# A node table filled by scatters from SBUF and loaded plainly, in place of an item table read by gathers

## The chip, the cores and the metric

The kernel runs on one core of a Trainium2 chip. The metric is the device time of one execution in microseconds (us). Five engines work side by side, each through its own list of instructions: TensorE (PE in the profile, its weight loads PEld), VectorE (DVE), ScalarE (ACT), GpSimd (POOL) and SyncE (SP). SP and ACT issue plain DMAs, POOL issues the indirect ones, in which a list of row numbers in SBUF picks the rows of a table in DRAM.

## What is computed

The reference is a chain of four layers on 3125 nodes with 256 features: a graph attention layer, a mixture of experts, a graph sum layer and an attention over slices. The change touches the second, and the first step of the third:

```python
x = x + _L0_gnn_ref(_layernorm(x), edge_index, ...)
x = x + _L0_ffn_ref(_layernorm(x)[None], router_w, w1, w2, w3)[0]
x = x + _L1_gnn_ref(_layernorm(x), L1_gnn_W, L1_gnn_b, edge_index)
x = x + _L1_ffn_ref(_layernorm(x)[None], ...)[0]

# _L0_ffn_ref, with 8 experts and the best 2 for each node
probs = softmax(flat @ router_w.T)
topk_probs, topk_idx = top_k(probs, 2)          # gates, made to sum to one
h = silu(flat w1[e]) * (flat w3[e])             # 682 wide
y = h w2[e]
out = sum over the two chosen e of gate[e] * y[e]
```

## The kernel before

Nodes are laid out as 25 tiles (`NT`) of 125 nodes (`P`), node = 125 x tile + partition. The residual stream `res` stays in SBUF. The phases follow one another, each a block with a barrier of all engines behind it: edges of the first graph layer, join, **router**, **experts**, **combine**, the sum over edges of the second graph layer, its node phase, and the last attention.

**Router** (`router_phase`). It normalises the nodes, stores the normalised rows to the DRAM table `xn_tab`, and chooses two experts for each node. Nodes are then grouped by expert into 56 items (`NI`) of 128 slots (`M`), an expert's last item being padded. `place[:, j, t]` is the slot of a node's j-th choice. From products of one-hot matrices, summed by TensorE in bank 2, VectorE makes `slot_token`, the node in each slot, in its last two instructions (L1461, L1462). 6250 of the 7168 slots hold a node.

**Experts** (`experts_phase`). GpSimd gathers the rows of each item from `xn_tab` into `e_x` (L1522, 56 indirect DMAs), with the first split of staged weights behind the sixteenth. A split (L1470, L1471) turns an expert's staged weights into a high and a low part; six more follow, each when a buffer is free. TensorE runs through the 56 items. At an item's end ScalarE copies the result from PSUM to one of two buffers `e_y` (L1645) and issues its store to the item table `y_tab` of 56 x 128 rows (L1647), 56 stores in all.

**Combine** (`combine_phase`). GpSimd clears a square, makes five small index rows (L842) and then issues 50 indirect DMAs (L1769): for each of 25 tiles and both choices the rows of `y_tab` at `place`, into `c_ys`. SP loads the last layer's weights (L1745 to L1756). VectorE clears the two halves of `sums` (L1784), then runs the walk (L869 to L896), small index work for the sum phase that has three products on TensorE in it, and then five groups of five tiles: wait for the group's ten gathers, ten multiply-adds into `res` (L1790), five statistics (L1793). Behind the fifth group come the normalising factors and 25 normalised tiles `c_xn` (L1254). SP stores them in five groups through `move` (L144, L145), which splits 125 partitions into 120 and 5. When they have landed, `close_layer` lets GpSimd clear the semaphores of the layer (L98), and the sum phase begins with its first gather (L930), the first of 392.

What a group of the combine stage waits for, and what it does:

```python
dve.wait_ge(ys_in[g], 16 * 2 * TB)
for j in range(2):
    for t in range(g * TB, (g + 1) * TB):
        m = v.scalar_tensor_tensor(out=k.res[:, t, :], in0=ys[:, j, t, :], scalar=k.gate[:, j, t:t + 1], in1=k.res[:, t, :], op0=ALU.mult, op1=ALU.add)
    me(dve, m)
```

The order on every engine is that of the code; no scheduler moves anything.

## Time and profile before

| what | us |
|---|---|
| median of 3 runs | 2197.47 (2193.42 to 2198.22) |
| the profiled execution, its own time | 2200.15 |
| its span, first to last instruction | 2198.4 |
| experts: first gather on GpSimd to last copy on ScalarE | 894.2 to 1307.2 |
| combine: first DMA on SP to the first gather of the sum phase | 1309.4 to 1403.6 |
| sum phase: first to last gather on GpSimd | 1403.6 to 1892.4 |

The span is cut by phases. Within a phase the question is which engine's list ends last, and what it waited for on the way. A row of a timeline gives the start of an instruction (or of a few merged ones) in us from the span's start, its length, the engine, the line in the kernel, what it writes and reads, how many were merged, and in square brackets how long the engine had idled before it and what ended that idle time. "issue" means that nothing which the profile shows was waited for. A Q behind an engine's name is its sequencer, which issues DMAs and sits at barriers.

### The profile page before, as it was taken

What the parts mean: (1) busy time and instruction counts of PE and PEld (TensorE: products, weight loads), DVE (VectorE), ACT (ScalarE), POOL (GpSimd) and SP (SyncE); (2) the same over time, 40 slices, a digit from 0 to 9 for tenths busy, and PEclk for the clock granted to TensorE, in tenths of its full rate; (3) what the DMA queues carried; (4) which work ended last, traced back from release to release, by engine and by line L of the source; (5) the groups of instructions that cost most, each with busy time, mean ns of one, the idle gap of its engine ahead of it and who ended that gap; (6) DMA issues with size and microseconds to landing.
All of it is one profiled execution on the core that took longest, in us unless ns stands there. A gap on an engine that the chain in (4) does not pass through costs nothing. (4 is left out here: it accounts for less than half of the span.)

```text
span 2198.4 us, 25811 instructions
## 1 busy us (share of the span) xinstructions
PE 1367.7 (62%) x6376; PEld 1110.0 (50%) x6377; DVE 955.0 (43%) x1910; ACT 447.7 (20%) x1239; POOL 1111.2 (51%) x1098
## 2 busy tenths in 40 slices
PE   2604676665652236798999971156656556477878
PEld 1403454544541225798999970134434444354557
DVE  8513544544434776432333335333323233365533
ACT  0213454444440011232333320000000000012210
POOL 4376777777746200574223117377777777303410
PEclk6756888777785665799999995577778787789979
DMA  5545889888878412242111023333333333100002
GB/s 131 141 119 160 295 301 312 283 279 264 282 236 180 42 40 59 88 154 96 60 60 60 21 63 104 108 105 105 105 105 105 105 105 105 57 1 0 0 0 59
DMA packets 151966, 268.97 MB, mean 122 GB/s; under 512 B 24036, under 2 KB 113476, under 8 KB 150763
## 3 DMA queue, kind: packets, MB, share of 16 engines
q0 software_dynamic: 46848, 127.07, 20.1%
q1 hardware_dynamic: 86760, 123.17, 17.1%
q10 hardware_dynamic: 18277, 17.70, 3.1%
q8 instruction: 44, 0.72, 0.1%
q14 instruction: 37, 0.30, 0.0%
HBM read 173.09 MB, written 94.74 MB: 122 GB/s over the span
## 5 line engine op out<-in xcount | busy, mean ns | idle before, releaser
L947 PE MATMUL bank<-sum_rows,sum_hot 128*125 x896 | 296.3, 496 | 281.6 <-SPq L921 216.3
L930 POOL DMA_INDIRECT sum_rows<-xn_tab,src_e x392 | 370.6, 945 | 148.3 <-issue 117.9
L721 POOL DMA_INDIRECT gat_rows<-xh_tab,src_e x364 | 344.3, 946 | 116.2 <-issue 107.5
L947 PEld LDWEIGHTS bank<-sum_rows,sum_hot 128*125 128x125 f32 x896 | 215.7, 251 | 362.3 <-issue 319.4
L778 PE MATMUL bank<-gat_rows,gat_same 128*128 128x264 f32 x784 | 255.4, 478 | 92.9 <-DVE gat_rows L754 92.9
L968 DVE TENSOR_TENSOR sums<-sums,bank 125x256 f32 x224 | 93.9, 421 | 348.9 <-PE bank L947 333.7
L778 PEld LDWEIGHTS bank<-gat_rows,gat_same 128*128 128x128 f32 x784 | 177.7, 241 | 131.7 <-issue 98.2
L1562 PE MATMUL bank<-weights,e_xthigh 128*128 x896 | 220.7, 330 | 11.1 <-POOL weights L1471 7.5
L800 ACT COPY gat_outs<-bank 128x264 f32<-128x264 f32 x392 | 148.4, 379 | 163.1 <-PE bank L778 150.4
L1691 DVE TENSOR_TENSOR e_h<-e_gated,bank 128x342 f32<-128x342 f32 x112 | 57.1, 510 | 269.2 <-ACT e_gated L1633 269.2
L1562 PEld LDWEIGHTS bank<-weights,e_xthigh 128*128 128x128 f32 x896 | 154.0, 192 | 20.6 <-issue 20.5
L1562 PE MATMUL bank<-weights,e_xtlow 128*128 x448 | 144.6, 323 | 0.0
L1583 PE MATMUL bank<-weights,e_hthigh 128*128 (+2 forms) x672 | 134.2, 296 | 0.2 <-DVE e_htlow L1696 0.2
L1220 ACT COPY n_xt<-bank 128x250 f32<-128x250 f32 x25 | 8.0, 372 | 572.0 <-PE bank L1207 571.6
L754 DVE TENSOR_TENSOR gat_rows<-gat_rows,bank 128x1792 f32<-128x1792 f32 x56 | 110.7, 2017 | 14.5 <-ACT bank L797 14.5
L1522 POOL DMA_INDIRECT e_x<-xn_tab,slot_token x56 | 54.6, 975 | 108.9 <-POOLq L1263 84.2
L1470 POOL CAST weights<-staged 128x4264 fp32r<-128x4264 f32 x7 | 26.3, 3758 | 153.0 <-SPq L1515 153.0
L1583 PEld LDWEIGHTS bank<-weights,e_hthigh 128*128 128x128 f32 (+2 forms) x672 | 103.1, 190 | 0.5 <-issue 0.4
L1633 ACT ACTIVATE e_gated<-bank 128x342 f32<-128x342 f32 x112 | 51.0, 455 | 245.2 <-PE bank L1562 245.2
L1583 PE MATMUL bank<-weights,e_htlow 128*128 x336 | 94.2, 280 | 0.0
L1562 PEld LDWEIGHTS bank<-weights,e_xtlow 128*128 128x128 f32 x448 | 86.0, 192 | 0.0
L1972 POOL TENSOR_TENSOR t_logit<-t_logit,t_peak 125x512 f32<-125x512 f32 x25 | 26.1, 1045 | 81.6 <-DVE t_peak L2131 81.6
(457 smaller groups left out, 2324.6 us busy)
## 6 DMA issues: line engine op xcount, KB each, us to landing
parts<-gat_outs SPq DMA_DIRECT2D x28, 1904.0 KB, 8.3
staged<-w_tab SPq DMA_DIRECT2D x8, 2132.0 KB, 8.4
w_tab<-w_stage SPq DMA_DIRECT2D x16, 682.0 KB, 10.6
w_raw<-in_L_ffn_w_dram SPq DMA_DIRECT2D x16, 640.0 KB
y_tab<-e_y ACTq DMA_DIRECT2D x56, 128.0 KB, 1.7
gat_rows<-xh_tab,src_e POOLq DMA_INDIRECT x392
sum_rows<-xn_tab,src_e POOLq DMA_INDIRECT x392, 2.7
w_tab<-w_stage SPq DMA_DIRECT2D x8, 768.0 KB
```

The source lines that it names most:

```text
L721: pool.indirect_dma_start(out=rows[b % R][:, t, :], out_offset=None, in_=k.xh_tab, in_offset=bass.IndirectOffsetOnAxis(ap=k.src_e[:, b * S ...
L754: v.tensor_tensor(f, f, weight[:, t0 * H:t1 * H].rearrange("p (t h a) -> p t h a", h=H, a=1).to_broadcast([EP, SB // 2, H, D]), ALU.mult). ...
L778: nc.tensor.matmul(k.ps[1 + (s * SB + t) % BK][:, 0:sums_w], same[s % 2][:, t, :], rows[s][:, t, 0:sums_w], start=True, stop=True).then_in ...
L800: nc.scalar.copy(outs[s % 2][:, t, 0:sums_w], k.ps[1 + (s * SB + t) % BK][:, 0:sums_w]).then_inc(taken, 1)
L930: pool.indirect_dma_start(out=rows[:, at // IP % (RING * GPAIRS), at % IP, :], out_offset=None, in_=k.xn_tab, in_offset=bass.IndirectOffse ...
L947: m = nc.tensor.matmul(k.ps[s][0:P, 0:C], hot[u][:, s, c, :], rows[:, bass.ds(slot, 1), c, :].rearrange("p a c -> p (a c)"), start=(c == 0 ...
L968: v.tensor_tensor(into, into, k.ps[s][0:P, 0:C], ALU.add).then_inc(added, 1)
L1522: pool.indirect_dma_start(out=x[:, i, :], out_offset=None, in_=k.xn_tab, in_offset=bass.IndirectOffsetOnAxis(ap=k.slot_token[:, i:i + 1], ...
L1562: last = nc.tensor.matmul(bank[:, 0:HH[a]], xt[s][px][:, c, :], part(slot, up_at(m, pw, c) + HB[a], 128, HH[a]), start=(n == 0), stop=(n = ...
L1583: m = nc.tensor.matmul(DOWN[s][:, 0:C], ht[a][ph][0:rows, b, :], part(slot, down_at(pw, 3 * a + b), rows, C), start=(a == 0 and n == 0), s ...
L1633: nc.scalar.activation(gated[a][:, 0:HH[a]], UP[a][:, 0:HH[a]], ACT.Silu).then_inc(silued, 1)
L1691: v.tensor_tensor(h[a][:, 0:HH[a]], gated[a][:, 0:HH[a]], GATE[a][:, 0:HH[a]], ALU.mult).then_inc(h_made, 1)
```

## The change

The item table becomes a node table of two rows for each node: row n for the first choice of node n, row 3125 + n for the second. The router makes a second list from the same products, `slot_row`, the node-table row of each slot. For that the second choice's column numbers run on from 25, the lane number goes in plus one (`row1`), so that an empty slot is told by zero, and five more VectorE instructions turn the sum into both lists. An empty slot gets a row number beyond the table. In the experts phase ScalarE copies an item's result over the item's own input `x[:, i, :]`; it issues no store. GpSimd scatters the 56 items to the node table behind its last split, and SP waits for all of them before the phase ends. In the combine phase SP loads the first choices and ACT the second ones, in five groups each, plainly; GpSimd clears `sums` where VectorE did.

```diff
-    k.xn_tab, k.y_tab = k.dram("xn_tab", [N, C]), k.dram("y_tab", [NI * M, C])
+    k.xn_tab, k.y_tab = k.dram("xn_tab", [N, C]), k.dram("y_tab", [2 * N, C])
...
+            me(dve, v.tensor_scalar(row1[:, :], k.node[:, 0:1], 1.0, None, ALU.add))
...
-                me(dve, v.tensor_scalar(at_item[:, at, 1, :], of_place[:, :, :], k.node[:, 0:1], None, ALU.mult))
+                me(dve, v.tensor_scalar(at_item[:, at, 1, :], of_place[:, :, :], row1[:, 0:1], None, ALU.mult))
...
-            me(dve, v.scalar_tensor_tensor(out=k.slot_token[:, :], in0=k.ps[2][:, 0:NI], scalar=float(P), in1=token[:, :], op0=ALU.mult, op1=ALU.add))
+            me(dve, v.scalar_tensor_tensor(out=token[:, :], in0=k.ps[2][:, 0:NI], scalar=float(P), in1=token[:, :], op0=ALU.mult, op1=ALU.add))
+
+            me(dve, v.tensor_scalar(second[:, :], token[:, :], float(N) + 0.5, -float(N), ALU.is_gt, ALU.mult))
+            me(dve, v.scalar_tensor_tensor(out=second[:, :], in0=token[:, :], scalar=-1.0, in1=second[:, :], op0=ALU.add, op1=ALU.add))
+            me(dve, v.tensor_scalar(k.slot_token[:, :], second[:, :], 0.0, None, ALU.max))
+            me(dve, v.tensor_scalar(second[:, :], token[:, :], 0.5, 4.0 * N, ALU.is_lt, ALU.mult))
+            me(dve, v.scalar_tensor_tensor(out=k.slot_row[:, :], in0=token[:, :], scalar=-1.0, in1=second[:, :], op0=ALU.add, op1=ALU.add))
...
+            sp.wait_ge(y_out, 16 * NI)
...
+            for i in range(NI):
+                pool.wait_ge(y_kept, i + 3)
+                pool.indirect_dma_start(out=k.y_tab, out_offset=bass.IndirectOffsetOnAxis(ap=k.slot_row[:, i:i + 1], axis=0),
+                                        in_=x[:, i, :], in_offset=None, bounds_check=2 * N - 1, oob_is_err=False).then_inc(y_out, 16)
...
-                if i >= 2:
-                    act.wait_ge(y_out[s], 16 * (i // 2))
-                nc.scalar.copy(y[s][:, :], DOWN[s][:, 0:C]).then_inc(y_kept, 1)
-                act.wait_ge(y_kept, i + 3)
-                act.dma_start(rows[i], y[s][:, :]).then_inc(y_out[s], 16)
+                nc.scalar.copy(x[:, i, :], DOWN[s][:, 0:C]).then_inc(y_kept, 1)
...
+            for g in range(GROUPS):
+                move(sp, ys[:, 0, g * TB:(g + 1) * TB, :], y_rows[:, 0, g * TB:(g + 1) * TB, :], ys_in[g])
...
-            for t in range(NT):
-                for j in range(2):
-                    pool.indirect_dma_start(out=picked[:, j, t, :], out_offset=None, in_=k.y_tab,
-                                            in_offset=bass.IndirectOffsetOnAxis(ap=k.places[:, j, t:t + 1], axis=0)).then_inc(ys_in[t // TB], 16)
+            for half in k.sums:
+                nc.gpsimd.memset(half[:, :, :], 0.0)
...
+            for g in range(GROUPS):
+                move(act, ys[:, 1, g * TB:(g + 1) * TB, :], y_rows[:, 1, g * TB:(g + 1) * TB, :], ys_in[g])
             norm_roots(k, act, deviations, roots)
...
-            for half in k.sums:
-                v.memset(half[:, :, :], 0.0)
             k.walk.on_vector(dve)
             for g in range(GROUPS):
-                dve.wait_ge(ys_in[g], 16 * 2 * TB)
+                dve.wait_ge(ys_in[g], 64)
```

GpSimd's list, from its last split in the experts phase to the first gathers of the sum phase, before:

```order
L1470 CAST weights<-staged 128x4264
L1471 TENSOR_TENSOR weights<-staged,weights 128x4264
L1481 UNCONDITIONAL_BRANCH
L1763 UNCONDITIONAL_BRANCH
L1765 MEMSET att_square 128x512
L842 IOTA walk_bound 24x1
L842 IOTA walk_pair_row 128x196
L842 IOTA walk_item_row 128x224
L842 IOTA walk_item_col 110x2
L842 IOTA walk_pair_col 98x2
L1769 DMA c_ys<-y_tab,place 128x256 x50
```

and the same stretch now:

```order
L1477 CAST weights<-staged 128x4264
L1478 TENSOR_TENSOR weights<-staged,weights 128x4264
L1538 DMA y_tab<-e_x,slot_row 6250x256 x56
L1488 UNCONDITIONAL_BRANCH
L1769 UNCONDITIONAL_BRANCH
L1771 MEMSET att_square 128x512
L842 IOTA walk_bound 24x1
L842 IOTA walk_pair_row 128x196
L842 IOTA walk_item_row 128x224
L842 IOTA walk_item_col 110x2
L842 IOTA walk_pair_col 98x2
L1774 MEMSET sums 125x6400 x2
```

The 56 scatters stand between the last split and the barrier (the two branches), and two clears stand where 50 gathers stood. On SP the combine phase began, before, with

```order
L1740 UNCONDITIONAL_BRANCH
L1745 DMA att_w_x<-in_L_ffn_W_x_dram 128x2x512
L1745 DMA att_w_fx<-in_L_ffn_W_fx_dram 128x2x512
L1745 DMA att_w_out<-in_L_ffn_W_out_dram 128x4x256
L1746 DMA att_b_fx<-in_L_ffn_b_fx_dram 1x512
```

and it begins now with

```order
L1744 UNCONDITIONAL_BRANCH
L144 DMA c_ys<-y_tab 120x5x256
L145 DMA c_ys<-y_tab 5x5x256
...
L144 DMA c_ys<-y_tab 120x5x256
L145 DMA c_ys<-y_tab 5x5x256
L1751 DMA att_w_x<-in_L_ffn_W_x_dram 128x2x512
L1751 DMA att_w_fx<-in_L_ffn_W_fx_dram 128x2x512
```

with five such pairs ahead of the weights; ACT has five pairs too, ahead of its square root. The end of the router on VectorE was

```order
L1459 TENSOR_SCALAR load_after<-r_sums 1x8
L1461 COPY r_token<-bank 128x56
L1462 SCALAR_TENSOR_TENSOR slot_token<-bank,r_token 128x56
```

and is

```order
L1460 TENSOR_SCALAR load_after<-r_sums 1x8
L1462 COPY r_token<-bank 128x56
L1463 SCALAR_TENSOR_TENSOR r_token<-bank,r_token 128x56
L1465 TENSOR_SCALAR r_second<-r_token 128x56
L1466 SCALAR_TENSOR_TENSOR r_second<-r_token,r_second 128x56
L1467 TENSOR_SCALAR slot_token<-r_second 128x56
L1468 TENSOR_SCALAR r_second<-r_token 128x56
L1469 SCALAR_TENSOR_TENSOR slot_row<-r_token,r_second 128x56
```

five rows longer, with both lists made in it. The semaphores that GpSimd clears behind the combine phase are 53, from 50.

## Rows read from the trace of the kernel before

**Rows 1.** Instruction groups by line, 1309 to 1404: busy, mean ns | idle before, releaser.

```profile
L1769 POOL DMA_INDIRECT c_ys<-y_tab,place x50 | 48.5, 970 | 15.1 <-issue 15.1
L1790 DVE SCALAR_TENSOR_TENSOR res<-c_ys,gate,res 125x256 f32<-125x256 f32 x50 | 20.7, 480 | 20.1 <-DMA c_ys<-y_tab,place 19.9
```

**Rows 2.** Timeline of VectorE in the combine phase.

```profile
1322.83 0.29 DVE L869 TENSOR_SCALAR walk_past<-bank,walk_bound 24x196 f32<-24x196 f32 x1
...
1328.60 0.27 DVE L886 CAST walk_pair_i<-walk_pair 1x224 int32<-1x224 f32 x1
...
1332.57 4.17 DVE L1790 SCALAR_TENSOR_TENSOR res<-c_ys,gate,res 125x256 f32<-125x256 f32 x10
...
1338.42 4.16 DVE L1790 SCALAR_TENSOR_TENSOR res<-c_ys,gate,res 125x256 f32<-125x256 f32 x10
...
1376.14 4.17 DVE L1790 SCALAR_TENSOR_TENSOR res<-c_ys,gate,res 125x256 f32<-125x256 f32 x10 [6.75 <-DMA c_ys<-y_tab,place]
...
1382.03 0.08 DVE L463 MEMSET rstd<- 125x25 f32 x1
```

**Rows 3.** GpSimd's gathers of the sum phase: ns min/median/max, first and last start.

```profile
L930 POOL DMA_INDIRECT sum_rows<-xn_tab,src_e x392: 942/946/962, 1403.6 to 1892.4; - x196
```

**Rows 4.** Timelines of SP, TensorE and GpSimd as the combine phase begins.

```profile
1309.42 0.40 SPq L1745 DMA_DIRECT2D att_w_x<-in_L_ffn_W_x_dram  x1
...
1309.48 1.65 PE L851 MATMUL bank<-dst_e,ident 128*128 128x392 f32 x2 [2.69 <-PEq L1481]
...
1310.63 0.13 POOL L842 IOTA walk_pair_col<- 98x2 f32 x1
```

**Rows 5.** Tile view of `adst_edge`: an earlier phase's 25 scatters, with bounds.

```profile
L611 POOL DMA_INDIRECT adst_edge<-xh,start_row x25: 1188/1189/2167, 96.3 to 133.2; - x25
...
DMA to landing us min/median/max: 2.4/3.8/7.3
```

**Rows 6.** GpSimd's last instruction of the experts phase, in its timeline.

```profile
1209.49 9.37 POOL L1471 TENSOR_TENSOR weights<-staged,weights 128x4264 fp32r<-128x4264 f32 x1
```

**Rows 7.** Tile view of `e_y`: the copies of the 56 results on ScalarE.

```profile
L1645 ACT COPY e_y<-bank x56: 372/373/376, 915.6 to 1306.8; 128x256 f32<-128x256 f32 x56
```

**Rows 8.** Timeline of ScalarE: the last copy and the last store of the experts phase.

```profile
1306.83 0.37 ACT L1645 COPY e_y<-bank 128x256 f32<-128x256 f32 x1 [2.16 <-PE bank L1583]
1307.23 0.33 ACTq L1647 DMA_DIRECT2D y_tab<-e_y  x1
```

**Rows 9.** DMA view: issues, KB each, median us to landing.

```profile
y_tab<-e_y ACTq DMA_DIRECT2D x56, 128.0 KB, 1.7
```

**Rows 10.** Timeline of VectorE at the end of the router.

```profile
892.54 0.22 DVE L1461 COPY r_token<-bank 128x56 f32<-128x56 f32 x1
892.79 0.22 DVE L1462 SCALAR_TENSOR_TENSOR slot_token<-bank,r_token 128x56 int32<-128x56 f32 x1
```

**Rows 11.** DMA view of 8 to 24, `res` loaded: packets, MB, share of 16 engines.

```profile
q10 hardware_dynamic: 2861, 2.89, 95.5%
```

**Rows 12.** Windows: us, busy of PE, PEld, DVE, ACT, POOL; PEclk, DMA share, GB/s.

```profile
1389.00:1392.00 3.00, 0.00 (x0) 0.00 (x0) 2.99 (x10) 0.00 (x0) 0.00 (x0) 0.50 0.97 310
```

**Rows 13.** Timeline of the first phase: two clears by GpSimd.

```profile
0.81 0.52 POOL L289 MEMSET srcq_i<- 98x512 int32 x1 [0.29 <-POOLq L2257]
1.27 0.52 POOL L290 MEMSET dstq_i<- 98x512 int32 x1
```

**Rows 14.** Timeline of the attention phase: VectorE beside GpSimd, and apart from it.

```profile
2006.45 1.29 DVE L1254 TENSOR_SCALAR t_xn<-res,mv,rstd 125x256 f32 x1 [0.15 <-issue]
2006.55 1.04 POOL L1976 TENSOR_TENSOR t_logit<-t_logit,t_total 125x512 f32<-125x512 f32 x1
...
2069.12 0.41 DVE L1254 TENSOR_SCALAR t_xn<-res,mv,rstd 125x256 f32 x1
```

**Rows 15.** Timeline of the spread phase: scans on VectorE, gathers on GpSimd.

```profile
145.78 9.04 DVE L654 TENSOR_TENSOR_SCAN filled<-cont_q,sparse 98x512 f32<-98x512 f32 x8
...
148.06 1.93 POOL L618 DMA_INDIRECT gat_rows<-xh_tab,src_e  x1 [0.30 <-issue]
```

18 lines of the change are left out of this document (7 added, 11 removed).

## The prediction

> **What bounds the kernel now.** I began with the stages in time, then asked in each stage that the diff touches which list ends last. The groups by line of the combine stage show GpSimd issuing 50 gathers and VectorE's 50 multiply-adds idle for 20.1 us, 19.9 of it for those gathers [rows 1]. One gather costs 0.97 us busy and 0.30 idle, (48.5 + 15.1) / 50 = 1.27 us, so ten for a group cost 12.7 us, against 1338.42 - 1332.57 = 5.85 us of VectorE work for a group [rows 1, 2]. From the third group on the stage goes at GpSimd's pace; its fifth group starts at 1376.14 and ends at 1382.03 [rows 2]. Ahead of the groups VectorE clears the two halves of `sums`, and the walk begins only at 1322.83, 13.4 us after the stage's first DMA [rows 2, 4]. The phases stand behind one another, and the sum phase is one row of 392 gathers at GpSimd's pace, (1892.4 - 1403.6) / 391 = 1.25 us each [rows 3]; it doesn't shorten, but it starts as much earlier as the combine stage ends, and so does all that follows. What is won between 1309 and 1382 is won in the total, unless the router or the experts phase gives it back.
>
> **The combine stage.** All 50 gathers go. The clears go from VectorE to GpSimd. The walk needs the index rows (ready at 1310.76) and the first product (1309.48 + 1.65 = 1311.13) [rows 4], so its first step can start at 1311.2 in place of 1322.83: 11.6 us earlier.
>
> GpSimd clears 2 x 6400 numbers a partition beside the walk. Its rate is in two clears of 512 that start 0.46 us apart [rows 13]: 6400 x 0.46 / 512 = 5.75 us each, from 1310.8 to 1322.3. Does VectorE work on beside them? One VectorE instruction took 1.29 us in place of 0.41, and ended at 2007.74, 0.15 after a GpSimd instruction that ran from 2006.55 to 2007.59 [rows 14]. So a GpSimd instruction can hold VectorE until its own end. In the walk the candidates are five short steps from the cast on (L886), which read and write SBUF with one operand and no PSUM. Moved up by 11.6 the cast comes at 1317.0, after the second clear has begun at about 1316.5; held, it goes on at 1322.3, 5.3 us later. That is a bound from above; the bound from below is 0, since the row is of a GpSimd instruction that reads SBUF, and a clear doesn't. I take the 5.3: it is the only case in these rows of long GpSimd work beside such steps.
>
> The Trainium skill states this as a rule (SBUF — State Buffer, section "Who interferes with whom"): a VectorE copy, cast or scalar operation in a two-port mode and any GpSimd instruction exclude each other, and the one issued second waits for the whole of the first. By it the 5.3 us are due; by the same page VectorE instructions with two SBUF inputs are held only by GpSimd work that reads, so the multiply-adds would not be. The trace agrees for [rows 14]; for a clear no row shows it.
>
> So the first group starts at 1332.57 - 11.6 + 5.3 = 1326.3, and five groups at VectorE's pace end at 1326.3 + 5 x 5.85 = 1355.5, if the rows are there. They are 2 x 3.2 = 6.4 MB, loaded plainly in pieces of 1 KB by SP and ACT. The nearest row is the load of `res`, of the same shape and through the same helper: 2.89 MB in 16 us with the 16 engines 95.5% busy, 181 GB/s [rows 11]. At that the last group lands at 1309.4 + 2 + 35.4 = 1346.8, ahead of 1326.3 + 4 x 5.85 = 1349.7, when VectorE asks for it. Stores of the same groups went at 310 GB/s [rows 12], which would land it at 1332. Either way the load is covered, down to 6.4 MB / 38.3 us = 167 GB/s. The last layer's weights now stand behind five pairs of loads on SP; they are not needed before the node phase, and SP's next timed duty, the store of the first normalised group, comes at about 1358. ACT's square root waits only for VectorE at 1356, behind its own five pairs. The combine stage thus ends 1382.03 - 1355.5 = 26.5 us earlier. Three more semaphores are cleared than the 50 of before. They are cleared somewhere between 1382.03 and 1403.6 [rows 2, 3], a stretch that is mostly normalising and storing: at most 3/50 of its 21.6 us, 1.3 us, at least nothing; I take 0.2.
>
> **The experts phase.** The 56 stores leave ScalarE, which is not late there, at no gain. The 56 scatters stand behind the last split, which ends at 1209.49 + 9.37 = 1218.9 [rows 6]. By then, at (1306.8 - 915.6) / 55 = 7.11 us an item [rows 7], some 43 of 56 results are made: GpSimd has a backlog. The one scatter in this trace, 25 times with bounds, takes 1.19 us [rows 5], with starts (133.2 - 96.3) / 24 = 1.54 us apart over all, the slow first one (2.17) included. 56 x 1.54 = 86.2 us, ending at 1305.1. The last result is copied at 1306.83 + 0.37 = 1307.2 [rows 8]. So the backlog is just gone, with 2 us to spare; the limit is (1307.2 - 1218.9) / 56 = 1.58 us a scatter. Bounds: 1.25 us, the gathers' pace [rows 3], and 1.93 + 0.30 = 2.23, which gathers took beside VectorE's scans [rows 15]. I take 1.54, as the nearest; VectorE's work in this phase has one operand in PSUM, and is no scan.
>
> Not hidden is the last scatter. Before, the store issued at 1307.23 landed 1.7 us later [rows 8, 9], 1308.9, and the next phase began at 1309.42. A scatter takes 2.4 to 7.3 us to landing, 3.8 in the middle [rows 5]: 1307.2 + 3.8 + 0.5 = 1311.5, 2.1 us later. From below 0.7; from above 5.6, where the backlog is not quite gone or the queue is full.
>
> **The router.** Five VectorE instructions behind the list's last one, at 892.79 - 892.54 = 0.25 us apart [rows 10], and one more near its start: 1.5 us, all on the path, since the experts phase begins with the gathers that read the list. The other edits there change numbers, not instructions.
>
> **Sum.** -26.5 + 2.1 + 1.5 + 0.2 = -22.7 us. The profiled execution's own time is 2200.15, which makes 2177.5; it lies 2.7 above the median of the runs, 2197.47. From the median: 2197.5 - 22.7 = 2174.8.
>
> **The rivals.**
> A: the clears hold nothing. For it: a clear reads nothing. Then the first group starts at 1321.0, the groups could end at 1350.2, and by the load at 181 GB/s the fifth starts at 1346.8 and ends at 1352.7. Saved are 29.3 to 31.8, less 3.8: 2166 to 2172 (some 2170).
>
> B: the load becomes the bound. For it: two queues ask for rows of one table at once, and [rows 11] has the engines at 95% already at 181 GB/s. At three quarters of it, 136 GB/s, the load takes 47 us, the fifth group starts at 1358.5 and ends at 1364.4: 17.6 saved, less 3.8, 2183.7. Against it: the 310 GB/s of [rows 12], with the same groups.
>
> C: GpSimd doesn't keep pace. Each 0.1 us a scatter over 1.58 adds 5.6 us to the experts phase. At 1.7 the total is 2181.5.
>
> D, the other side: the same mechanism far enough. At 2.23 us a scatter [rows 15] GpSimd ends at 1218.9 + 124.9 = 1343.8 and the phase at about 1346: it starts the combine stage 34 us later than my forecast has it, which is 2209, 12 us slower than before. It decides from 1.58 + 22.7 / 56 = 1.99 us on. Against it: the gathers of the same phase ran beside the same VectorE work at no visible cost.
>
> E: the change doesn't do what it says, because VectorE waits elsewhere or the sum phase starts late for a reason that I don't see: within 0.2%.
>
> **How the numbers follow.** Forecast 44%, A 27%, B 12%, C 8%, D 5%, E 4%. The range: from 2164, A at its best with the runs' own spread of some 2 us, to 2184, B at three quarters. It leaves out D, E and the far parts of B and C. 0.2% is 4.4 us, about what a measurement of this kernel can tell from no change. Faster by more: forecast, A, B and most of C, 0.90; within it: E, 0.04; slower: D and a little, 0.06.
>
> **What would show it.** In the profile after: scatters 1.5 us apart from 1220 to 1305, the last one waiting for ScalarE; combine's first DMA at about 1313 (1309.4 + 1.5 + 2.1); the walk's first step 2 us behind it, and the cast (L886) late by some 5 us behind GpSimd's second clear; five groups 5.85 us apart with no wait for DMA; the sum phase's first gather at about 1381. It is wrong if the scatters end well behind ScalarE's last copy, if the groups wait for `c_ys`, or if the sum phase's gathers are no longer 1.25 us apart.

## The result: 5.4 us of a forecast 22.7

| | before | after |
|---|---|---|
| median of the runs, us | 2196.74 (12 runs, 2192.98 to 2199.21) | 2191.38 (12 runs, 2186.87 to 2197.60) |
| profiled execution, its own time / span | 2200.15 / 2198.4 | 2193.07 / 2191.3 |
| granted TensorE clock, mean | 0.781 | 0.784 |

The ratio is 0.9976, with a 95% interval from 0.9966 to 0.9986. The kernel became faster by a quarter of a percent; forecast were 2174.8 us and a range from 2164 to 2184. In the last three comparisons of the study the kernel before itself took 2528 to 2559 us, at a mean granted clock of 0.72 to 0.73, so the totals of those runs are set against that before alone and rank no cure, and their traces serve for durations, waits and the lengths of stages.

The two profiles differ by 7.1 us of span. Where they differ, in us from the span's start:

| event | before | after | difference of the stretch |
|---|---|---|---|
| first gather of the join stage | 663.8 | 669.2 | +5.4 |
| experts stage, ScalarE's first cast | 893.6 | 902.2 | +3.2 |
| ScalarE's last copy of a result ends | 1307.2 | 1314.8 | -1.0 |
| combine stage, SP's first DMA | 1309.4 | 1326.0 | +9.0 |
| first group of multiply-adds | 1332.6 | 1344.8 | -4.4 |
| fifth group's statistics end | 1382.0 | 1374.1 | -20.2 |
| first gather of the sum phase | 1403.6 | 1396.6 | +1.0 |
| end | 2198.4 | 2191.3 | -0.2 |

The combine stage has its gain: from its first DMA to the sum phase's first gather 94.1 us before, 70.6 now. But it begins 16.6 us later: 7.6 of these were lost ahead of the last copy, where the change has only the router's six instructions, and 9.0 between the last copy and the next stage.

VectorE in the combine stage of the kernel after, in its timeline (start us, duration us, engine, line, operation, [idle before <- releaser]); these rows answer to [rows 2], with L1794 for L1790:

```profile
1327.84 0.41 DVE L869 TENSOR_SCALAR walk_past<-bank,walk_bound 24x196 f32<-24x196 f32 x1 [14.95 <-PE bank L851]
...
1330.55 7.69 DVE L877 TENSOR_SCALAR walk_diag<-ident,walk_at 110x110 f32<-110x110 f32 x2
...
1344.83 4.17 DVE L1794 SCALAR_TENSOR_TENSOR res<-c_ys,gate,res 125x256 f32<-125x256 f32 x10
...
1350.69 4.16 DVE L1794 SCALAR_TENSOR_TENSOR res<-c_ys,gate,res 125x256 f32<-125x256 f32 x10
...
1368.21 4.15 DVE L1794 SCALAR_TENSOR_TENSOR res<-c_ys,gate,res 125x256 f32<-125x256 f32 x10
...
1374.08 0.08 DVE L463 MEMSET rstd<- 125x25 f32 x1
```

The groups run 5.83 to 5.86 us apart, and the fifth has no wait in brackets, where [rows 2] had 6.75 us of it. The walk begins 1.8 us behind the stage's first DMA, as forecast. One pair of its steps, L877, takes 7.69 us; in other runs below it takes 0.46.

GpSimd from its last split through the stage's start. The scatters (L1538) answer to [rows 5], the index rows to [rows 4]:

```profile
1216.85 9.37 POOL L1478 TENSOR_TENSOR weights<-staged,weights 128x4264 fp32r<-128x4264 f32 x1
1226.38 1.04 POOL L1538 DMA_INDIRECT y_tab<-e_x,slot_row  x1 [0.17 <-issue]
1227.72 1.00 POOL L1538 DMA_INDIRECT y_tab<-e_x,slot_row  x1 [0.30 <-issue]
...
1291.64 0.97 POOL L1538 DMA_INDIRECT y_tab<-e_x,slot_row  x1 [0.31 <-issue]
1298.19 0.97 POOL L1538 DMA_INDIRECT y_tab<-e_x,slot_row  x1 [5.58 <-ACT e_x L1653]
1305.26 0.97 POOL L1538 DMA_INDIRECT y_tab<-e_x,slot_row  x1 [6.09 <-ACT e_x L1653]
1312.01 0.97 POOL L1538 DMA_INDIRECT y_tab<-e_x,slot_row  x1 [5.78 <-ACT e_x L1653]
1315.62 0.97 POOL L1538 DMA_INDIRECT y_tab<-e_x,slot_row  x1 [2.63 <-ACT e_x L1653]
1326.05 0.53 POOL L1771 MEMSET att_square<- 128x512 f32 x1 [9.46 <-POOLq L1488]
...
1327.14 0.13 POOL L842 IOTA walk_item_col<- 110x2 f32 x1
1327.24 0.13 POOL L842 IOTA walk_pair_col<- 98x2 f32 x1
1327.32 5.42 POOL L1774 MEMSET sums<- 125x6400 f32 x1
```

The scatters go 1.28 us apart, 52 of them follow each other without a wait, the backlog is worked off at 1292.6, and the last four wait for ScalarE, each behind its own result. The costly row is the first of L1771: L1488 is the block of the experts stage, POOLq GpSimd's sequencer, and between the end of the last scatter, 1316.59, and the next stage lie 9.46 us. The waits of SP say who was late there (waited for: us in total, times, longest us):

```profile
SPq L1488 <- DMA y_tab<-e_x,slot_row: 104.7, 1, 104.7
SPq L1488 <- PEq L1488: 8.1, 1, 8.1
```

SP waited for the scatters to land, and then 8.1 us more at the end of the block for the other engines. So the rows had landed at 1326.0 - 8.1 = 1317.9, some 2 us behind the issue of the last scatter. It wasn't the data that was late. Nor was it TensorE, whose last product ended at 1314.4, or ScalarE, whose last row is:

```profile
1314.47 0.37 ACT L1653 COPY e_x<-bank 128x256 f32<-128x256 f32 x1 [2.23 <-PE bank L1594]
```

The router's five added steps, behind the one of [rows 10], which is now the first row here:

```profile
900.19 0.22 DVE L1463 SCALAR_TENSOR_TENSOR r_token<-bank,r_token 128x56 f32<-128x56 f32 x1
900.44 0.19 DVE L1465 TENSOR_SCALAR r_second<-r_token 128x56 f32<-128x56 f32 x1
...
901.37 0.22 DVE L1469 SCALAR_TENSOR_TENSOR slot_row<-r_token,r_second 128x56 int32<-128x56 f32 x1
```

And the gathers of the edge phase, whose code is the same in both kernels, first before and then after (ns min/median/max, first and last start us):

```profile
L721 POOL DMA_INDIRECT gat_rows<-xh_tab,src_e x364: 942/946/1022, 183.8 to 637.7; - x182
```

```profile
L721 POOL DMA_INDIRECT gat_rows<-xh_tab,src_e x364: 952/957/1048, 183.8 to 641.6; - x182
```

Each takes 11 ns longer at the median, and the quickest 10 ns. It is the same for the other gathers ahead of the experts stage, 471 with these 364 (25 of windows, 28 in the spread phase, 50 in the join stage; the other 4 of the spread phase take 3 ns more); the 25 scatters of L611 take what they took. From the experts stage on both kernels have 946 again, the 392 gathers of the sum phase (L930) too: 1396.6 to 1885.6, 489.0 us, as in [rows 3].

So three things were to be explained: who holds the walk, why GpSimd is late at the end of the experts stage, and why gathers ahead of any change are slower. All kernels that were run for it, each with the ratio to before in the same comparison:

| kernel | median us (runs) | before there | ratio, 95% interval |
|---|---|---|---|
| after_last_two | 2188.87 (7) | 2195.68 | 0.9956 (0.9941 to 0.9972) |
| after_small_clears | 2196.82 (12) | 2195.68 | 1.0005 (0.9994 to 1.0016) |
| before_row_tile | 2197.03 (11) | 2195.68 | 1.0003 (0.9994 to 1.0012) |
| after_old_table | 2191.01 (8) | 2195.68 | 0.9976 (0.9964 to 0.9988) |
| before_end_gather | 2202.14 (12) | 2198.48 | 1.0023 (1.0013 to 1.0032) |
| before_end_scatter | 2205.89 (6) | 2198.48 | 1.0038 (1.0023 to 1.0053) |
| last_two_late_clears | 2184.59 (6) | 2198.48 | 0.9944 (0.9929 to 0.9958) |
| last_two_act_clears | 2184.42 (6) | 2198.48 | 0.9939 (0.9924 to 0.9955) |
| after_spare_rows | 2564.11 (6) | 2527.71 | 1.0149 (1.0116 to 1.0183) |
| late_clears_spare_rows | 2550.90 (6) | 2527.71 | 1.0092 (1.0063 to 1.0122) |
| after_late_clears | 2550.62 (8) | 2527.71 | 1.0086 (1.0058 to 1.0115) |
| before_end_scatter_free | 2523.21 (12) | 2527.71 | 0.9979 (0.9961 to 0.9997) |
| after_late_clears, second time | 2594.98 (4) | 2558.16 | 1.0152 (1.0128 to 1.0175) |
| last_two_first | 2585.04 (4) | 2558.16 | 1.0108 (1.0085 to 1.0131) |
| after_last_28 | 2555.56 (12) | 2558.16 | 0.9993 (0.9978 to 1.0008) |
| before_end_narrow | 2566.00 (12) | 2558.16 | 1.0039 (1.0018 to 1.0061) |
| after_late_clears, third time | 2594.97 (5) | 2558.51 | 1.0154 (1.0136 to 1.0173) |
| before_node_scatter | 2558.02 (10) | 2558.51 | 0.9997 (0.9984 to 1.0010) |

The last ten rows say something against the change. Every kernel in them that issues 54 or 56 scatters behind the last split took 0.9 to 1.5% longer than before, though its combine stage is as short as in the other traces. The traces place it in the experts stage, while the backlog of scatters goes out. Windows of that time (us, then busy us of PE, PEld, DVE, ACT and POOL with instructions, PEclk, DMA share, GB/s), of the kernel after, and of after_late_clears, third time:

```profile
1226.00:1285.00 59.00, 59.00 (x421) 57.20 (x421) 20.47 (x60) 20.08 (x68) 45.06 (x47) 1.00 0.26 92
```

```profile
1442.00:1500.00 58.00, 18.11 (x90) 15.87 (x89) 3.70 (x11) 3.39 (x11) 43.12 (x45) 0.60 0.26 91
```

Beside the same stream of scatters TensorE is busy all the time in the one, and 18.1 of 58.0 us in the other, idle at "issue", that is, for nothing that the profile shows, once for 14.9 us. The DMA engines moved 91 GB/s beside it, against 92. The granted clock was 1.00 (2.4 GHz) until 1453, with TensorE idle since 1450, and 0.50 (1.2 GHz) for the rest of the window. Eight results took 109 us there in place of 56, and the stage from its first gather to its last copy 502 us; it took 449 to 456 us in the three kernels of these rows with one scatter or none in it, and 465 in after_last_28 with 28. Why TensorE idles, no run shows, and the kernel after itself wasn't among these runs; after_late_clears differs from it in the place of the clears alone.

### The profile page after: what moved, and what is told of

It is laid out like the page before. It is cut to its first block and busy times, and to the rows that moved or that the text cites. A ratio compares the mean times of both kernels' runs of the same rounds, so it can differ in the third digit from the quotient of the medians.

```text
span 2191.3 us, 25791 instructions
## 1 busy us (share of the span) xinstructions
PE 1364.0 (62%) x6376; PEld 1106.4 (50%) x6377; DVE 955.0 (44%) x1914; ACT 448.0 (20%) x1239; POOL 1131.9 (52%) x1106
## 5 line engine op out<-in xcount | busy, mean ns | idle before, releaser
L930 POOL DMA_INDIRECT sum_rows<-xn_tab,src_e x392 | 370.8, 946 | 177.7 <-issue 116.7
L721 POOL DMA_INDIRECT gat_rows<-xh_tab,src_e x364 | 348.2, 957 | 116.2 <-issue 107.9
L1573 PEld LDWEIGHTS bank<-weights,e_xthigh 128*128 128x128 f32 x896 | 153.9, 192 | 20.3 <-issue 20.2
L1538 POOL DMA_INDIRECT y_tab<-e_x,slot_row x56 | 54.6, 974 | 35.8 <-ACT e_x L1653 20.1
```

The source lines that it names most:

```text
L721: pool.indirect_dma_start(out=rows[b % R][:, t, :], out_offset=None, in_=k.xh_tab, in_offset=bass.IndirectOffsetOnAxis(ap=k.src_e[:, b * S ...
L930: pool.indirect_dma_start(out=rows[:, at // IP % (RING * GPAIRS), at % IP, :], out_offset=None, in_=k.xn_tab, in_offset=bass.IndirectOffse ...
L1538: pool.indirect_dma_start(out=k.y_tab, out_offset=bass.IndirectOffsetOnAxis(ap=k.slot_row[:, i:i + 1], axis=0), in_=x[:, i, :], in_offset= ...
L1573: last = nc.tensor.matmul(bank[:, 0:HH[a]], xt[s][px][:, c, :], part(slot, up_at(m, pw, c) + HB[a], 128, HH[a]), start=(n == 0), stop=(n = ...
```

## Experiments on the end of the experts stage

**after_last_two** issues the last two scatters in the next stage, ahead of the clears; SP and ScalarE wait for them there before their first loads:

```diff
-            for i in range(NI):
-                pool.wait_ge(y_kept, i + 3)
-                pool.indirect_dma_start(out=k.y_tab, ...
+            for i in range(NI - 2):
+                pool.wait_ge(y_kept, i + 3)
+                scatter(pool, i)
 ...
             k.walk.on_pool(pool)
+            k.last_rows(pool)
+            nc.gpsimd.memset(k.att["square"][:, :, :], 0.0).then_inc(squares0, 1)
 ...
+            act.wait_ge(k.y_out, 16 * NI)
             for g in range(GROUPS):
                 move(act, ys...
```

> The kernel after, with the scatters of the last two items moved behind the walk's index rows in the combine stage (SP's and ScalarE's loads there wait for them, and the experts stage ends when 54 have landed). In after the combine stage begins 11.2 us behind ScalarE's last copy, though the DMA queues are silent from 2.8 us behind it on. Theory 1, what is late is GpSimd itself, at the end of a block that it leaves behind an indirect DMA: with its last scatter of the block 7 us ahead of the last copy, the combine stage begins about 2 to 3 us behind the last copy, its loads start 3.5 to 5 us behind its own start, and the total falls by 9 less up to 2.6, by which the clears come later and let the walk go later: 2182 to 2186. Theory 2, a scatter's completion comes late: the combine stage begins as early, but its loads start 10 to 12 us behind its start; the total is then 2185 to 2192. Theory 3, the late start has nothing to do with the scatters: the stage still begins 11 us behind the last copy, 2191 or more.

ScalarE's last copy and GpSimd's timeline there:

```profile
1310.66 0.37 ACT L1659 COPY e_x<-bank 128x256 f32<-128x256 f32 x1 [2.16 <-PE bank L1600]
```

```profile
1301.51 0.97 POOL L1540 DMA_INDIRECT y_tab<-e_x,slot_row  x1 [6.03 <-ACT e_x L1659]
1311.79 0.12 POOL L842 IOTA walk_bound<- 24x1 f32 x1 [9.31 <-POOLq L1488]
```

The stage now begins 0.8 us behind the end of the last copy, 1311.03, in place of 11.2, and GpSimd shows 9.31 us between its last scatter and the stage, though its rows had landed 7.1 us before the stage. Its loads start at 1316.16, 4.4 us behind the stage's start: theory 1; a slow completion (theory 2) would have put them at 1322 or later. The stage itself is 73.2 us long in place of 70.6, since the clears come 2.4 us later. Expected were 2182 to 2186 us, measured 2188.87, with a profiled run of 2186.44: the trace has the mechanism, the median gives back less of it, and the interval of its ratio overlaps with that of after (0.9966 to 0.9986).

Is it any indirect DMA, or a scatter? Two kernels add one instruction to the kernel before, behind ScalarE's last copy, which SP waits for. **before_end_gather**:

```diff
+            pool.wait_ge(y_kept, NI + 2)
+            pool.indirect_dma_start(out=x[:, 0, :], out_offset=None, in_=k.xn_tab,
+                                    in_offset=bass.IndirectOffsetOnAxis(ap=k.slot_token[:, NI - 1:NI], axis=0)).then_inc(tail, 16)
```

> The kernel before, with one more gather on GpSimd at the end of the experts block: it waits for ScalarE's last copy, reads 128 rows of xn_tab into a tile that nothing reads any more, and SP waits for it. In after the next stage began 9.5 us behind the end of GpSimd's last scatter, in after_last_two 9.3 us. Theory 1, GpSimd takes some 9 us to leave a block behind any indirect DMA: the gather ends at about 1308.3, the combine stage begins at about 1317.7 in place of 1309.4, total 8 us over before, 2204. Theory 2, about 5 us, as behind the spread stage's gathers (178.2 to 183.8): 1313.5, total 2200. Theory 3, only scatters cost it: the stage waits for the landing alone and begins at about 1311, total 2197 to 2198.

**before_end_scatter**:

```diff
+            pool.wait_ge(y_kept, NI + 2)
+            pool.indirect_dma_start(out=k.spare_tab, out_offset=bass.IndirectOffsetOnAxis(ap=k.slot_token[:, NI - 1:NI], axis=0),
+                                    in_=y[(NI - 1) % 2][:, :], in_offset=None, bounds_check=N - 1, oob_is_err=False).then_inc(tail, 16)
```

> The same with a scatter in place of the gather: the last item's result to a spare table of 1 KB rows that nothing reads, with bounds. Theory 1 and theory 3: the combine stage begins at about 1317.8. It also asks why every indirect DMA ahead of the experts stage takes 957 ns in after and 946 in before, with tiles and tables in the same place or not: if a scatter of 1 KB rows somewhere in the program does it, the edge phase's gathers (L721) take 957 ns here too and the total is 2208 to 2209; if it is another part of the change, 946 ns and 2204.

GpSimd's timeline in the one and in the other:

```profile
1308.88 0.98 POOL L1532 DMA_INDIRECT e_x<-xn_tab,slot_token  x1 [88.77 <-ACT e_y L1650]
1315.06 0.53 POOL L1770 MEMSET att_square<- 128x512 f32 x1 [5.20 <-POOLq L1481]
```

```profile
1314.08 1.04 POOL L1533 DMA_INDIRECT spare_tab<-e_y,slot_token  x1 [89.14 <-ACT e_y L1651]
1320.10 0.53 POOL L1771 MEMSET att_square<- 128x512 f32 x1 [4.97 <-POOLq L1482]
```

Neither theory 1 (9 us) nor theory 3 (scatters alone) stands: one indirect DMA as GpSimd's last work of the block costs some 5 us, be it a gather (5.20) or a scatter (4.97). What makes 9.46 of it? **after_spare_rows** takes away the bounds and the rows that they leave out: it gives each empty place a row of its own behind the table.

```diff
-            me(dve, v.tensor_scalar(second[:, :], token[:, :], 0.5, 4.0 * N, ALU.is_lt, ALU.mult))
+            me(dve, v.scalar_tensor_tensor(out=second[:, :], in0=token[:, :], scalar=0.5, in1=spare[:, :], op0=ALU.is_lt, op1=ALU.mult))
 ...
-                                        in_=x[:, i, :], in_offset=None, bounds_check=2 * N - 1, oob_is_err=False).then_inc(y_out, 16)
+                                        in_=x[:, i, :], in_offset=None).then_inc(y_out, 16)
```

> The kernel after, where the rows of empty places (some 16 of 128 an item) go to rows of their own behind the table's 6250 in place of being left out by the bounds, so that the scatters need no bounds. GpSimd needed 9.46 us to leave the block in after and 9.31 in after_last_two, but 5.20 behind one gather at the end and 4.97 behind one scatter with bounds and no row out of them. Theory 1, the bounds or the rows left out make the difference: here the leaving takes about 5.0 us, the combine stage begins 4.4 us earlier, and if bounds also make the indirect DMAs ahead of the experts stage slow (957 ns), these take 946 again, 5 us more: 2182 to 2187. Theory 2, the number of scatters does it: 9.4 us, 957 ns, 2191.

```profile
1558.05 0.96 POOL L1540 DMA_INDIRECT y_tab<-e_x,slot_row  x1 [2.57 <-ACT e_x L1655]
1568.47 0.53 POOL L1773 MEMSET att_square<- 128x512 f32 x1 [9.46 <-POOLq L1490]
```

9.46 us to the hundredth: bounds have no part in it. late_clears_spare_rows (below) has the same change. **after_last_28** halves the number. ScalarE's plain stores fill the table's rows before that, and the routed rows of the first 28 items are left out of the result:

```diff
-            for i in range(NI):
+            pool.wait_ge(filled, 16 * 49)
+            for i in range(28, NI):
                 pool.wait_ge(y_kept, i + 3)
 ...
+                if i < 28:
+                    act.wait_ge(y_kept, i + 3)
+                    for at in (i, i + 28):
+                        rows = min(M, 2 * N - at * M)
+                        if rows > 0:
+                            act.dma_start(k.y_tab[at * M:at * M + rows, :], x[0:rows, i, :]).then_inc(filled, 16)
```

> The kernel after, in which GpSimd scatters the last 28 items alone; the rows of the first 28 are stored plainly by ScalarE into all of the table's rows before that, 49 stores, so that the routed rows of these items are left out of the result. GpSimd leaves the block in 9.46 us behind 56 scatters, in 9.31 behind 54, in 4.97 behind one: (9.46 - 4.97) / 55 = 0.082 us a scatter. Theory 1, it goes with the number of scatters: here 4.97 + 27 x 0.082 = 7.2 us. Theory 2, it goes with what the last few did (their spacing and their rows are as in after): 9.4 us.

```profile
1542.41 0.97 POOL L1539 DMA_INDIRECT y_tab<-e_x,slot_row  x1 [2.58 <-ACT e_x L1654]
1550.56 0.53 POOL L1778 MEMSET att_square<- 128x512 f32 x1 [7.17 <-POOLq L1488]
```

7.17 where 7.2 was expected. One scatter 4.97, 28 scatters 7.17, 54 scatters 9.31, 56 scatters 9.46: 4.9 us and 0.082 for each scatter of the block, an estimate from these four. Gathers don't count in this way: before_end_gather had 57 of them in the block, at 5.20. Nor is the count the whole rule: the spread phase has 25 scatters of 32-byte rows, with 28 gathers behind them, and leaves in 5.59. What GpSimd does in this time, no row shows.

## Experiments on the held walk

**after_small_clears** cuts each clear into 25 instructions:

```diff
             for half in k.sums:
-                nc.gpsimd.memset(half[:, :, :], 0.0)
+                for t in range(NT):
+                    nc.gpsimd.memset(half[:, t, :], 0.0)
```

> The kernel after, with GpSimd's two clears of 6400 numbers a partition cut into 50 clears of 256. Theory 1, a GpSimd clear holds a VectorE step of the walk until its own end (in after, L877 took 7.7 us in place of 0.5, up to the end of the second clear): a held step is let go after at most 0.3 us, the first group of multiply-adds starts about 12.5 us behind the stage's first DMA in place of 18.8, and the total is 5.5 to 6.5 us under after, about 2185. Theory 2, the walk is late for another reason (the loads' descriptors, or VectorE shares the port with whatever GpSimd writes, whole or in pieces): the first group still starts 17 to 19 us behind, total 2191.

VectorE's held step, and GpSimd's clears:

```profile
1330.99 9.62 DVE L877 TENSOR_SCALAR walk_diag<-ident,walk_at 110x110 f32<-110x110 f32 x2
```

```profile
1327.76 12.72 POOL L1775 MEMSET sums<- 125x256 f32 x50
```

My theory 1 falls in its detail. The step isn't let go at the end of the clear in hand, 0.25 us later, but at the end of the fiftieth: VectorE had no turn between clears that follow one another without a gap. The 50 take 12.7 us in place of 10.8, and the hold grows by these 1.9. (The trace explains 2.1 us of stage; the median is 5.4 over after's, and the rest isn't explained.) In the kernel after it was the same with two: L877 came at 1330.55 during the first clear and ended at 1338.2, with the second.

**last_two_late_clears** puts both clears behind the walk, on top of after_last_two:

```diff
+            pool.wait_ge(walked, 1)
             for half in k.sums:
                 nc.gpsimd.memset(half[:, :, :], 0.0)
```

> after_last_two with GpSimd's two clears behind the end of the walk, so that they lie beside the multiply-adds and statistics in place of the walk. There the walk's L877 was held for 11.4 us, until the second clear was through. Theory 1, multiply-adds and statistics are not held: the first group starts about 10.4 us behind the stage's first index row in place of 21.3, the fifth waits 1 or 2 us for its rows, total 9 to 10 us under after_last_two, 2179 to 2180. Theory 2, something in a group (the multiply-adds with a scale from SBUF, or the statistics) is held as L877 was, until both clears are through: the first group still starts early, but the second starts 6 to 11 us late, total 2183 to 2189.

VectorE's timeline, with GpSimd's clears below it:

```profile
1316.38 0.46 DVE L877 TENSOR_SCALAR walk_diag<-ident,walk_at 110x110 f32<-110x110 f32 x2
...
1326.47 4.17 DVE L1806 SCALAR_TENSOR_TENSOR res<-c_ys,gate,res 125x256 f32<-125x256 f32 x10 [3.06 <-DMA c_ys<-y_tab]
1330.67 1.73 DVE L1809 BATCH_NORM_STATS2 stats<-res 125x6 f32<-125x256 f32 x5
1333.14 4.17 DVE L1806 SCALAR_TENSOR_TENSOR res<-c_ys,gate,res 125x256 f32<-125x256 f32 x10 [0.73 <-DMA c_ys<-y_tab]
...
1352.02 4.17 DVE L1806 SCALAR_TENSOR_TENSOR res<-c_ys,gate,res 125x256 f32<-125x256 f32 x10 [0.81 <-DMA c_ys<-y_tab]
```

```profile
1323.52 10.81 POOL L1784 MEMSET sums<- 125x6400 f32 x2 [7.44 <-DVEq L1801]
```

L877 takes 0.46 us, and a group beside the clears takes as long as one without them, 4.17 and 1.73. So multiply-adds and statistics aren't held. But of the 10.1 us by which the walk ends earlier (21.3 to 11.1 us behind the stage's start) the stage keeps 4.9 (73.21 to 68.36 us from its start to the sum phase's first gather): groups now wait for their rows, 3.06, 0.73, 0.17 and 0.81 us. The last rows are there 35.4 us behind the first load, 6.4 MB at 181 GB/s. This is the load that [rows 11] gave, and it becomes the bound as soon as the walk no longer is. The total, 2184.59, is 4.3 us under after_last_two, where 9 to 10 were expected; by the ratios, 0.9944 and 0.9956 of their own before, it is 2.6 us, with intervals that overlap.

**last_two_act_clears** gives the clears to ScalarE:

```diff
+            for half in k.sums:
+                nc.scalar.mul(half[:, :, :].rearrange("p t c -> p (t c)"), k.ones[0:P, 0:1].to_broadcast([P, NT * C]), 0.0)
             norm_roots(k, act, deviations, roots)
```

> after_last_two with the two clears on ScalarE, behind its issues of loads (two multiplications by zero of 6400 numbers a partition, from one column of ones). ScalarE has nothing to do there until the square root. Theory 1, ScalarE holds nobody: the first group starts about 10.4 us behind the stage's first index row, the total is 9 to 10 us under after_last_two, 2179 to 2180, the same as last_two_late_clears at its best. Theory 2, the clears end behind the square root's turn (they begin only when the issues are through, some 24 us behind the stage's start): 2182 to 2186.

ScalarE cleared for 10.96 us, from 1339.69, and was through 12 us ahead of its square root. The total, 2184.42, is the same as with late clears, and for the same reason; the groups waited 3.03, 0.44, 1.17, 0.59 and 1.02 us for rows. Both are about 0.6% faster than before and a third of a percent faster than after; they are the best of this study.

**after_late_clears** has the late clears alone (the same edit, without the moved scatters), and was run three times:

> The kernel after, with GpSimd's clears behind the end of the walk and nothing else. The walk is let go 7.2 us earlier, the first group could start at about 1337.6. In last_two_late_clears, where the walk was through 8 us behind the first load, the groups then waited for their rows: 6.4 MB took 35.4 us, 181 GB/s. Theory 1: the first group starts 11.6 us behind the stage's first DMA or with a short wait, the fifth some 35.5 us behind it, and the gain over after is 6 to 7 us, 2184.5 to 2185.5. Theory 2, the loads' wait eats more than half of it: 2188 or more.

VectorE's held step in the first one's trace:

```profile
1581.74 0.47 DVE L877 TENSOR_SCALAR walk_diag<-ident,walk_at 110x110 f32<-110x110 f32 x2
```

This is the cleanest evidence on the walk, since nothing but the place of the clears differs from after, and the loads run beside the step as they do there: 0.47 us in place of 7.69, and as much in the two other traces. The first group starts at 1588.93, 11.7 us behind the stage's first DMA, with 0.16 us of wait; the fifth waits 0.57 us for its rows, and the sum phase begins 64.9 us behind the stage's start in place of 70.6 (64.4 and 64.5 in the others). Theory 1 has the walk right; what it is worth in a total isn't measured, since the three totals, 0.9 to 1.5% over before, are those of the stalled TensorE told above.

**last_two_first** is last_two_late_clears with the two scatters ahead of the index rows:

> last_two_late_clears (2184.6 us) with the last two scatters ahead of the walk's index rows on GpSimd in place of behind them. The loads, for which the first group there waited 3.06 us and later groups 1.7 more, start 0.9 us earlier; the walk starts 2.4 us later, which is less than that wait. Theory 1, the loads are what ends last: 0.9 us less, about 2183.7. Theory 2, the walk becomes it: 0 to 1 us more, 2185.

The first group waits 0.16 us there, and from ScalarE's last copy to the sum phase's first gather it takes 68.7 us in place of 69.1: less than half of the 0.9 that theory 1 had. The total, 1.0108 of before, says nothing of it.

**late_clears_spare_rows** adds the edit of after_spare_rows to last_two_late_clears:

> The same beside the two cures already run: last two scatters in the combine stage, clears behind the walk (last_two_late_clears, 2184.6 us), and no bounds. With the last two scatters moved the leaving is hidden at 9.3 us as at 5, so theory 1 gives only what the gathers ahead of the experts stage give back: 2180 if they take 946 ns again, 2184.6 if they stay at 957.

Its gathers ahead of the experts stage took 960 ns, so nothing was given back; its total, 1.0092 of before, is one of those with the stalled TensorE.

## Experiments on the gathers ahead of the change

**before_row_tile** is the kernel before with the tile that the change allocates; **after_old_table** is the kernel after with the table at its old length:

```diff
-    k.slot_token = k.sb("slot_token", [M, NI], I32)
+    k.slot_token, k.slot_row = k.sb("slot_token", [M, NI], I32), k.sb("slot_row", [M, NI], I32)
```

```diff
-    k.xn_tab, k.y_tab = k.dram("xn_tab", [N, C]), k.dram("y_tab", [2 * N, C])
+    k.xn_tab, k.y_tab = k.dram("xn_tab", [N, C]), k.dram("y_tab", [NI * M, C])
```

> The kernel before, with one thing of the change alone: the tile slot_row (56 numbers a partition) is allocated behind slot_token and never used, so that every tile behind it lies 224 bytes higher. In the profile after, the edge phase's gathers (L721) take 957 ns at the median mean in place of 946, the join phase starts 5.4 us later and the experts phase 8.6 us later, of which six VectorE instructions of the router explain 1.5. Theory 1, the place of the tiles in SBUF does it: here the gathers take 957 ns, the join phase starts at about 669 us in place of 663.8, the experts phase at about 900.5 in place of 893.6, and the total is 4 to 7 us over before (2201 to 2204). Theory 2, something else does it (the shorter table, or the code): 946 ns, 663.8 us, 893.6 us, and the total of before, 2197, within 2 us.

> The kernel after, with y_tab allocated at its old 7168 rows (the last 918 unused), so that the tables behind it in DRAM (dst_pad, start_tab, parts, chains) lie where they lay before. Theory 1 (place of the tiles in SBUF): nothing changes against after, gathers 957 ns, join phase at about 669, 2191 us. Theory 2 (place of the tables in DRAM): gathers 946 ns, join phase at about 664, experts phase at about 895, total 2185 to 2187.

The medians of L721 were 947 and 957 ns, the totals those of before and of after. Both theories fall: neither the place of the tiles nor that of the tables does it. before_row_tile shows something else. Its experts stage began at 897.5, 3.9 us later than in the profile of before, with quick gathers and the same median time. So of two single profiles some 2 to 4 us ahead of the experts stage mean nothing.

before_end_scatter (above) had 960 ns, and before_end_gather, with its gather in the same place, 946. One scatter at the end of the experts stage is enough, though the gathers that are slower with it run 576 to 1282 us ahead of it, so it can't be its transfer that slows them. **before_end_scatter_free** leaves out its bounds (its diff is against before_end_scatter), **before_end_narrow** takes rows of 8 numbers, and **before_node_scatter** has such a scatter in the node stage in place of the experts stage:

```diff
-                                    in_=y[(NI - 1) % 2][:, :], in_offset=None, bounds_check=N - 1, oob_is_err=False).then_inc(tail, 16)
+                                    in_=y[(NI - 1) % 2][:, :], in_offset=None).then_inc(tail, 16)
```

```diff
+            pool.indirect_dma_start(out=k.spare_tab, out_offset=bass.IndirectOffsetOnAxis(ap=k.slot_token[:, 0:1], axis=0),
+                                    in_=k.ones[:, 0:H], in_offset=None, bounds_check=N - 1, oob_is_err=False).then_inc(tail, 16)
+            pool.wait_ge(tail, 16)
```

> before_end_scatter without bounds on its one scatter. There the gathers ahead of the experts stage took 958 to 960 ns in place of 946, with nothing changed up to them, and the total was 7 us over before. Theory 1, a scatter with bounds on rows of 1 KB does it: here 946 ns, and a total some 4 to 5 us under before_end_scatter, 2201 to 2202. Theory 2, any scatter of such rows does it: 957 to 960 ns, 2206.

> before_end_scatter with rows of 32 bytes in place of 1 KB, into a spare table of 8 numbers a row. Theory 1, the length of the row makes the indirect DMAs ahead of the experts stage slow: here they take 946 ns, and the total is 4 to 5 us under before_end_scatter's 2206, at 2201 to 2202, as before_end_gather. Theory 2, any scatter in or behind the experts stage does it: 957 to 960 ns, 2206.

> The kernel before, with one scatter of 128 rows of 32 bytes on GpSimd in the node stage, behind the last gather of the program (its semaphore is waited for on GpSimd, beside the stage's weights). Theory 1, a scatter slows the indirect DMAs ahead of it in the program by some 11 ns each: here all of them, the 392 gathers of the sum stage (L930) among them, take 957 ns in place of 946, and the total is some 9 us over before. Theory 2, only those of the first layer's stages are slowed: 957 there and 946 from the experts stage on, total 5 us over before. Theory 3, it goes with the experts stage itself: 946 everywhere, total of before.

L721 (here L722) in before_end_narrow, and in before_node_scatter:

```profile
L722 POOL DMA_INDIRECT gat_rows<-xh_tab,src_e x364: 954/960/997, 197.2 to 778.5; - x182
```

```profile
L722 POOL DMA_INDIRECT gat_rows<-xh_tab,src_e x364: 940/946/957, 197.7 to 774.4; - x182
```

Without bounds it was 958 ns. So it is neither the length of the row nor the bounds, and a scatter behind the sum phase does nothing at all: theory 3 of the last one, it goes with a scatter in the experts stage. Other stages weren't tried, and this scatter differs from before_end_narrow's in its source and its index column too. What carries it from there to the gathers of the first layer, no run shows. It stays open, with its size known: in the edge phase the first to the last gather take 457.9 us in after and 458.5 in before_end_scatter, 453.9 in before. That is 3.9 us in after; the slower gathers ahead of the edge phase cost nothing, since it begins at 183.8 in both.

## Why the prediction missed, step by step

The sum was -26.5 + 2.1 + 1.5 + 0.2 = -22.7. The profiles give -7.1, the medians -5.4.

**The gathers that go, and the pace of a group: right.** The 50 gathers and VectorE's 19.9 us of waiting for them are gone, the groups go 5.83 to 5.86 us apart, and the walk starts 11.6 us earlier against the stage's start, as worked out.

**The load: right.** In the kernel after no group waits for rows, so rival B is out here; last_two_late_clears shows how near the bound was, with the 181 GB/s of [rows 11].

**The hold of VectorE: right in kind, wrong in place and size.** The working let the five short steps from the cast on (L886) be held, by 5.3 us. Held was L877, 7.2 us (7.69 less 0.46), so rival A is out. The step that failed is the list of candidates, "five short steps from the cast on": L877 also reads one operand from SBUF and writes SBUF, and it comes beside the first clear. The Trainium skill (SBUF — State Buffer, section "Who interferes with whom") would have pointed at it: it names copies, casts and `tensor_scalar` as the operations that can take the shared pair of ports, and leaves out the form that writes its accumulator. The trace agrees: L873, of that form, ran in 0.41 us beside the same clear, L877 didn't. It says that who issues first has the ports for the whole instruction; here they were had for a whole run of instructions, 2 or 50 of them, as long as they followed without a gap. The mis-sizing is worth 1.9 us.

**The end of the combine stage: 0.2 forecast, 1.0 measured** (1374.08 to 1396.63 in place of 1382.03 to 1403.56).

**The pace of the scatters: on the good side.** I took 1.54 us, and 1.25 as a bound; measured are 1.28. GpSimd was through with its backlog at 1292.6, 22 us ahead of the last result. Rivals C and D are out.

**The last scatter: wrong, the dearest term.** Forecast was "1307.2 + 3.8 + 0.5", 2.1 us later than before; measured are 9.0. The landing was even quicker than taken, some 2 us. What the step left out is the engine itself. Before, GpSimd ended its work of this block 88 us ahead of ScalarE's last copy; after the change it is the last one to leave. The price of leaving was in the profile of before, where GpSimd ends the spread phase with gathers:

```profile
177.26 0.95 POOL L618 DMA_INDIRECT gat_rows<-xh_tab,src_e  x1 [0.30 <-issue]
183.80 0.94 POOL L721 DMA_INDIRECT gat_rows<-xh_tab,src_e  x1 [5.59 <-POOLq L585]
```

5.59 us from the last gather to the next phase's first instruction, released by the sequencer of its own block. I counted what the change adds to GpSimd's list and not what it puts at its end. With this row the last scatter, ending at 1309.0, would have put the next stage at 1314.5, 5.1 us later than before; the other 3.9 of the 9.0 go with the number of scatters, which no row of before shows.

**The router: right.** Five steps from 900.44 to 901.59 are 1.15 us, with the sixth about 1.4; forecast 1.5.

**What the sum didn't have.** The gathers of the edge phase, which the change doesn't touch, cost 3.9 us more, by a cause that is only placed, not explained. Of the rest of what is lost ahead of the experts stage, 8.6 - 1.5 - 3.9 = 3.2 us, before_row_tile says that it is no more than executions differ by.

Together: 6.9 (leaving) + 3.9 (gathers) + 1.9 (hold) + 0.8 (stage's end) + 3.2 (unassigned) - 1.0 (experts stage, 413.6 to 412.7 us, and roundings) make 15.7 of the 15.6 us by which the profiles fell short. The case that came is, in kind, rival E: the sum phase starts late for reasons that I didn't see. With 0.24% it lies just beyond E's 0.2%. It had 4 in 100, and the range ended at 2184 where the runs have 2191.4. It was too narrow because each of its bounds was one of a cost that I had named. Its lower end has a slip besides: rival A's best is 2197.5 - 31.8 + 3.8 = 2169.5, not 2166; nothing hangs on it.

## What to carry to other kernels

When work is added at the end of an engine's list, look at what that engine does between its last instruction and the next stage wherever it already ends a stage in that way: here GpSimd needed some 5 us behind an indirect DMA, and some 0.08 more for each scatter of the block. With two scatters moved into the next stage that stage began 0.8 us behind the last copy in place of 11.2, and its loads 5.1 us behind it. And a clear on GpSimd isn't free beside VectorE: here it cost nothing beside multiply-adds and statistics, or on ScalarE, and much beside a `tensor_scalar` step, in pieces or whole. When both cures are in, ask again what is late next: here it was the load, which took back half of what the walk had gained. Last, work that is hidden behind TensorE in one trace need not be so in the next: the scatters that cost the experts stage nothing in the result's comparison cost it some 50 us in three others.

## What the runs showed of the hardware that was not expected

- GpSimd leaves a block late behind indirect DMAs: 5.20 us behind a gather, 4.97 behind one scatter, 7.17 behind 28, 9.31 behind 54, 9.46 behind 56, the same with and without bounds, and with the rows of after landed 8.1 us before.
- GpSimd's clears hold a VectorE `tensor_scalar` through a whole run of instructions: L877 was held 9.6 us by 50 clears of 0.25 us each.
- Beside back-to-back scatters TensorE was busy for 59.0 of 59.0 us in after, and for 18.1 of 58.0 in after_late_clears, third time, waiting for nothing that the profile shows.
- With a scatter at the end of the experts stage the gathers that run 576 to 1282 us ahead of it in before_end_scatter take 11 to 14 ns longer (957 to 960 in place of 946), with long rows or short, with bounds or without; with one in the node stage they don't.
- A scatter of 128 rows of 1 KB with bounds takes 0.97 us on GpSimd, 1.28 from one to the next, close to a gather's 0.95 and 1.25; the 25 scatters of [rows 5] took 1.19.
